# Attention and two feed-forward layers on one core: the last sixteen tiles' steps written in another order on all five engines

## The reference

```
def _layer(x, wqkv, qs, ksc, wo, lg, lb, w1, b1, w2, b2):
    h = shift_token(x)                      # half of the columns taken from the row before
    q, k, v = split(h @ wqkv)               # 256 -> 3 x 512, 8 heads of 64
    q, k = l2norm(q) * qs, l2norm(k) * ksc
    q, k = rotary_xpos(q, k)
    o = local_attention(q, k, v)            # window of 128 rows, and the window before
    x = x + o @ wo
    h = layernorm(shift_token(x)) * lg + lb
    a, g = split(h @ w1 + b1)               # 256 -> 2 x 682
    return x + (a * gelu(g)) @ w2 + b2
x = layernorm(x + attention(x)); y = x
for l in range(2): y = _layer(y, ...)
return layernorm(x + y)
```

## Time and profile before

| | us |
|---|---|
| median of 3 runs (smallest to largest) | 2690.54 (2689.98 to 2692.51) |
| the profiled execution: its time, its span | 2691.48, 2689.7 |
| TensorE busy | 2630.9 (98%) |
| VectorE busy | 2275.5 (85%) |
| ScalarE busy | 1934.2 (72%) |
| GpSimd busy | 1658.0 (62%) |
| `last_steps` on TensorE | from 2402.3 to 2684.8 |

### The profile page before, as it was taken

The page is one execution under the profiler, slowest core; times in us unless marked ns, Lnnn a source line. Parts: engine busy times, 40 slices in busy tenths (PEclk is TensorE's granted clock), DMA queues, the critical chain, the costliest instruction groups (busy, mean ns, idle before and its releaser), DMA issues. The chain is left out here.

```text
span 2689.7 us, 65519 instructions
## 1 busy us (share of the span) xinstructions
PE 2630.9 (98%) x22240; PEld 2317.6 (86%) x22240; DVE 2275.5 (85%) x6866; ACT 1934.2 (72%) x4826; POOL 1658.0 (62%) x1753
## 2 busy tenths in 40 slices
PE   8999999999999999999999999999999999999998
PEld 6677788899999899999998988989898998988887
DVE  5778888888888888888887889888989989998786
ACT  5655588777777777777776777777777777778775
POOL 6533755566566566566555676666766667766563
PEclk9999899999999999999999999999999999999999
DMA  9931200000000000000012211111110111111110
GB/s 315 341 100 54 107 21 25 28 28 25 29 25 25 28 24 29 27 27 25 28 39 90 89 36 34 33 33 37 35 32 30 37 33 37 30 36 34 30 32 23
DMA packets 144510, 140.37 MB, mean 52 GB/s; under 512 B 16024, under 2 KB 126128, under 8 KB 143408
## 3 DMA queue, kind: packets, MB, share of 16 engines
q1 hardware_dynamic: 144176, 136.18, 16.0%
HBM read 80.02 MB, written 51.92 MB: 49 GB/s over the span
## 5 line engine op out<-in xcount | busy, mean ns | idle before, releaser
L954 POOL TENSOR_TENSOR prob<-prob,rinv 128x512 f32<-128x512 f32 (+1 forms) x512 | 506.1, 1000 | 396.4 <-DVE rinv L1760 396.1
L1218 ACT ACTIVATE prob<-prob,least 128x256 f32<-128x256 f32 (+1 forms) x1024 | 495.8, 486 | 62.4 <-DVE least L1752 60.9
L932 POOL TENSOR_TENSOR inv_norm<-norm_clipped,minus_half 128x8 f32<-128x8 f32 x256 | 422.7, 1658 | 79.5 <-DVE norm_clipped L1718 72.1
L1752 DVE CUSTOM_DVE_ANT_0 prob<-p_pair,mask,inv_norm 128x256 f32<-128x256 f32 (+1 forms) x1024 | 440.2, 459 | 35.1 <-PE p_pair L176 33.2
L174 PE MATMUL p_pair<-hT_h,w_h 128*128 128x256 f32 (+1 forms) x1408 | 413.4, 294 | 8.5 <-DVE gated L1824 3.6
L176 PE MATMUL p_pair<-hT_h,w_l 128*128 128x256 f32 (+1 forms) x1408 | 394.9, 280 | 0.0
L175 PE MATMUL p_pair<-hT_l,w_h 128*128 128x256 f32 (+1 forms) x1408 | 394.5, 280 | 0.0
L1230 ACT ACTIVATE pT<-p_turn 128x512 f32<-128x512 f32 (+1 forms) x512 | 283.5, 569 | 76.6 <-PE p_turn L2529 64.1
L174 PE MATMUL p_pair<-wqkv_h,xT_h 128*128 128x512 f32 x768 | 329.6, 429 | 6.5 <-DVE rope_sin L1702 2.6
L176 PE MATMUL p_pair<-wqkv_h,xT_l 128*128 128x512 f32 x768 | 305.6, 398 | 0.0
L175 PE MATMUL p_pair<-wqkv_l,xT_h 128*128 128x512 f32 x768 | 304.6, 397 | 0.0
(11 more groups left out here) (129 smaller groups left out, 7577.4 us busy)
## 6 DMA issues: line engine op xcount, KB each, us to landing
x_tile<-x_rows SPq DMA_DIRECT2D x192, 128.0 KB, 2.1
a_wraw<-in_w_all SPq DMA_DIRECT2D x32, 264.0 KB, 5.3
w_high<-a_wraw_h SPq DMA_DIRECT2D x32, 264.0 KB, 3.9
w_low<-a_wraw_l SPq DMA_DIRECT2D x32, 264.0 KB, 4.4
a_x<-in_x SPq DMA_DIRECT2D x32, 256.0 KB, 4.2
x_rows<-a_x SPq DMA_DIRECT2D x64, 128.0 KB, 2.0
x_tile<-x_rows SPq DMA_DIRECT2D x128, 64.0 KB, 2.0
mid_rows<-x_mid SPq DMA_DIRECT2D x128, 64.0 KB, 1.7
```

What stands on the lines that cost most here:

```text
L932: pool.tensor_tensor(r[:, t.slot(2), heads], rt[:, heads], half[:, heads], ALU.pow).then_inc(pool_r[n], 1)
L954: pool.tensor_tensor(p, p, rinv[:, 2 * m:2 * m + 2].unsqueeze(2).to_broadcast([P, 2, cols.stop - cols.start]), ALU.mult).then_inc(pool_p, 1)
L1218: act.activation(prob[:, h, cols], prob[:, h, cols], ACT.Exp, bias=least[:, h:h + 1], scale=-1.0, accum_out=rsum[:, h:h + 1]).then_inc(act ...
L1752: dve.tensor_tensor_reduce(prob[:, h, cols], p_score[h % 2][:, c0 + cols.start:c0 + cols.stop], mask[:, a.slot(2), cols], r[:, a.slot(2), ...
```

## The change

The calls inside the five `last_steps` lists are written in another order. Each engine has the same calls with the same arguments as before (69 on SP, 154 on POOL, 346 on ACT, 506 on DVE, 300 on PE), and the waits (`after`) on PE move with their calls, some of them naming another step that now precedes. The beginning and the loop are untouched. The first few calls of each list are the same; the first one that differs on PE is the 43rd. The diff is some 2,300 lines long, and three pieces of it follow. On SP, the first one:

```diff
@@ -842,8 +842,8 @@
             load_x1(T(117))
             store_x(T(112))
             store_x(T(113))
+            load_x(T(120))
             store_mid(T(116))
-            load_x(T(120))
             load_shifted(T(116))
             load_x1(T(118))
             store_mid(T(117))
...
```

On DVE near the end:

```diff
             gated_low(Q(122), 5)
-            least_of(T(127), 0)
-            least_of(T(127), 1)
-            least_of(T(127), 2)
-            least_of(T(127), 3)
-            o_low(T(126))
-            x_new(T(122))
-            final_statistics(T(122))
-            least_of(T(127), 4)
-            least_of(T(127), 5)
-            inverse_sums(T(127), 0)
-            least_of(T(127), 6)
-            final(T(122))
-            least_of(T(127), 7)
-            x_new(T(123))
-            final_statistics(T(123))
-            inverse_sums(T(127), 1)
-            final(T(123))
-            middle(T(126))
-            h_affine(Q(124))
-            h_low(Q(124))
-            statistics(T(126))
-            o_low(T(127))
             normed(T(126))
             gated(Q(124), 0)
             gated(Q(124), 1)
-            middle(T(127))
+            x_new(T(122))
+            final_statistics(T(122))
+            statistics(T(127))
+            gated(Q(124), 2)
+            final(T(122))
+            x_new(T(123))
+            normed(T(127))
             gated_low(Q(124), 0)
+            final_statistics(T(123))
+            gated(Q(124), 3)
             gated_low(Q(124), 1)
-            gated(Q(124), 2)
             gated_low(Q(124), 2)
-            gated(Q(124), 3)
-            statistics(T(127))
+            h_affine(Q(126))
             gated_low(Q(124), 3)
             gated(Q(124), 4)
+            final(T(123))
             gated(Q(124), 5)
-            normed(T(127))
+            h_low(Q(126))
             gated_low(Q(124), 4)
             gated_low(Q(124), 5)
-            h_affine(Q(126))
-            h_low(Q(126))
+            gated(Q(126), 0)
             x_new(T(124))
...
```

On PE, around the place to which the output product of tile 127 has come (its own new line stands just ahead of the piece):

```diff
-            after((dve_oT, T(127), 1, 1))
-            output(T(127))
+            after((dve_gT, Q(122), HF + 1, 6))
+            narrow(T(122))
             after((dve_gt, Q(124), HF + 1, 1))
             widen(Q(124), 2)
             after((dve_gt, Q(124), HF + 1, 2))
             widen(Q(124), 3)
+            after((dve_x, T(122), 1, 1))
+            narrow(T(123))
             after((dve_gt, Q(124), HF + 1, 3))
             widen(Q(124), 4)
+            after((dve_hn, T(127), 1, 1))
+            turn_h(Q(126))
             after((dve_gt, Q(124), HF + 1, 4))
             widen(Q(124), 5)
-            after((dve_hn, T(127), 1, 1))
-            turn_h(Q(126))
-            after((dve_hv, Q(126), 1, 1))
-            narrow(T(124))
             after((dve_hT, Q(126), 1, 1))
             widen(Q(126), 0)
+            after((dve_gT, Q(124), HF + 1, 6))
+            narrow(T(124))
             after((dve_gt, Q(124), HF + 1, 6))
             widen(Q(126), 1)
+            after((dve_gt, Q(126), HF + 1, 1))
+            widen(Q(126), 2)
             after((dve_x, T(124), 1, 1))
             narrow(T(125))
-            after((dve_gt, Q(126), HF + 1, 1))
-            widen(Q(126), 2)
             after((dve_gt, Q(126), HF + 1, 2))
             widen(Q(126), 3)
             after((dve_gt, Q(126), HF + 1, 3))

...
```

More of the change, by code:

```diff
@@ L1482, in last_steps @@
             v_out(T(122))
[L1483 to L1497 removed]
+            k_high(T(122))
@@ L2107, in last_steps @@
             q_low(T(120))
             inverse_sums(T(119), 1)
-            gated(Q(116), 0)
+            rope_cos(T(121), 0)
+            norms(T(121), 0)
             x_new(T(114))
+            rope_sin(T(121), 0, 0)
+            clip(T(121), 0)
+            rope_sin(T(121), 0, 1)
             final_statistics(T(114))
+            q_sum(T(121))
+            k_low(T(120))
+            x_new(T(115))
+            final(T(114))
+            final_statistics(T(115))
+            h_affine(Q(116))
+            final(T(115))
@@ L2177, in last_steps @@
             least_of(T(121), 7)
-            gated(Q(116), 5)
-            h_affine(Q(118))
-            gated_low(Q(116), 5)
-            o_low(T(120))
-            h_low(Q(118))
+            k_low(T(122))
+            q_low(T(122))
+            x_new(T(116))
+            inverse_sums(T(121), 1)
+            final_statistics(T(116))
             rope_cos(T(123), 1)
@@ L2903, in last_steps @@
             turn_k(T(119))
+            after((act_v, T(119), 1, 1))
+            widen(Q(114), 1)
+            after((dve_mid, T(116), 1, 1))
+            turn_x(T(120))
             after((dve_gt, Q(114), HF + 1, 1))
@@ L3147, in last_steps @@
             turn_probs(T(122), 3)
+            after((act_pT, T(122), 4, 3))
+            values(T(122), 2)
+            after((dve_kr, T(124), 1, 1))
+            project_v(T(124))
             after((dve_q, T(124), 1, 1))
@@ L3263, in last_steps @@
             turn_probs(T(125), 1)
-            after((dve_mid, T(124), 1, 1))
-            turn_x(T(127))
+            after((act_pT, T(125), 4, 1))
+            after((pool_p, T(125), 4, 3))
+            turn_probs(T(125), 2)
+            after((dve_kr, T(127), 1, 1))
+            project_v(T(127))
+            after((dve_x, T(119), 1, 1))
+            turn_h(Q(122))
+            after((dve_kT, T(126), 1, 1))
+            scores(T(126), 0)
+            after((dve_q, T(127), 1, 1))
+            after((act_pT, T(125), 4, 3))
@@ L3321, in last_steps @@
             turn_probs(T(126), 0)
+            after((dve_gt, Q(120), HF + 1, 4))
+            widen(Q(120), 5)
+            after((dve_oT, T(125), 1, 1))
+            after((act_pT, T(126), 4, 1))
+            values(T(126), 0)
+            after((dve_oT, T(125), 1, 1))
+            output(T(125))
+            after((dve_kT, T(127), 1, 1))
+            scores(T(127), 0)
             after((dve_kT, T(127), 1, 1))
@@ L3376, in last_steps @@
             values(T(127), 3)
+            after((dve_gt, Q(122), HF + 1, 3))
+            widen(Q(122), 4)
+            after((dve_gt, Q(122), HF + 1, 4))
+            widen(Q(122), 5)
+            after((dve_oT, T(127), 1, 1))
+            output(T(127))
             after((dve_hT, Q(124), 1, 1))
```

1489 lines of the change are left out of this document (731 added, 758 removed).

## The result

The changed kernel takes 2696.07 us (median of 22 runs, 2689.8 to 2704.05), the kernel before 2690.43 (22 runs, 2687.49 to 2700.89). The ratio is 1.0018, with a 95% interval of 1.0011 to 1.0025: slower, by about 4.8 us, which is just under the 5.4 us that I had called the least a measurement can tell.

A forecast was written before the change was run, and what follows sets the result against it. TensorE, busy 2630.9 of 2689.7 us, bounds the kernel, so only its waits change. From the profiled 2691.48, +1.0 at the end and +0.5 in the middle give 2693.0, or 2692.0 against the median; range 2683.5 to 2699.

The forecast's parts named there:

- What bounds the kernel: Whole kernel: TensorE is busy 2630.9 of 2689.7 us, so a new order can only win back its waits.
- The end, covered turn_h, late h_low: After output(127): turn_h(126) no longer waits, widen(126,0) loses 3.35 us for h_low; 7.3 us lost against 7.1, +0.2.
- The clock at the end: After output(127): idle may halve TensorE's clock, adding 1.6 us (+1.8 in all); the middle, +1.0, was taken.
- The middle, +0.5: Tiles 112 to 127: one-hop shortfalls say +1.4 us, the saved wait for x takes 1.0 back; +0.5 likeliest.
- The wait on the transfer: turn_x(122) waits 0.86 us for x of tile 122; more TensorE work in between would save about 1.0.
- three places that I named: Middle, predicted shortfalls: probs_out(118) 1.64, project_v(122) behind gated(116,5) 1.24, project_v(125) behind v_out(124) and a squares 1.51 us.
- the count of one hop: Middle: TensorE work between dependent calls less the shortest hand-over; shortfalls sum to 4.8 us old, 6.2 new, so +1.4.
- the 13 that I had named as the sign of being wrong: TensorE idle up to output(127), before 9.2 us: above 13 (slower) or under 5 (faster) makes the prediction wrong.
- The factor of 2.5: Middle: queues adding to each other as before, 12.1 / 4.8, turn 6.2 into 15.6 us, so +3.5.
- my slow rival: ScalarE's queue at gelu(114,4) makes shortfalls compound by 2.5 or more, clock lowered at the end: 2696 to 2699; chance 0.20.
- Two loads out of the full stretch: Middle: gelu(114,4) and (114,5) share a table load; two loads leave ScalarE's crowded stretch, 2.6 us of its time.
- Theory A: From the experiments: each long wait is one call too far back in a queue; over a microsecond also lowers the clock.

The follow-up runs named there:

- e3: Kernel after with tile 119's x_low ahead of q_sum(118) and a clip on VectorE, and the end reordered on TensorE, VectorE and ScalarE; ratio 1.0011 to before.
- e7: Kernel after with GpSimd's k_sum of tile 118 cut from 128x512 to 128x64; one profile, last steps 292.0 us against 293.25 in the kernel after.
- e5: Kernel after with three exp calls moved on ScalarE (tile 120's 6 and 7, tile 123's 0), so four table loads go; ratio 1.0008 to before.
- e9: Kernel after with tile 119's x_low earlier, the end reordered, three exp calls moved, and nine more calls moved on VectorE and ScalarE; ratio 1.0008 to before.
- e1: Kernel after with one VectorE call moved: tile 119's x_low ahead of q_sum(118) and a clip; ratio 1.0020 to before.
- e2: Kernel after with narrow(123) and turn_h(126) earlier on TensorE and the calls around them on VectorE and ScalarE reordered; ratio 1.0019 to before.
- e10: Kernel before with middle(118), x_low(127) and h_affine(122) moved earlier on VectorE; ratio 0.9993 to before.
- e11: Kernel after with tile 119's x_low earlier, end reordered, three exp calls moved, and gated(116,5) and least_of(125,1) to (125,3) earlier on VectorE; ratio 0.9998 to before.

## Why the prediction was right, and which terms were off

- *What bounds the kernel.* Right: TensorE has the same work, and the change shows in its waits and, which the sum had at the end alone, in its clock.
- *The end, covered turn_h, late h_low.* The mechanism was right call by call: 0.9 us predicted before widen(124,5), 0.92 lost; 3.35 before widen(126,0), 2.88 lost; normed(127) behind x_new(123) in time. h_low started at 15.5 us after output(127) (2666.39 - 2650.89), predicted 15.85. e3 shows that VectorE's and TensorE's order there made it.
- *The clock at the end.* I took half of 1.6 us. It fell, and cost 2.75, because the slow stretch was 6 us long and not 3.3. The end came out at +2.4 instead of +1.0: a term mis-sized. The Trainium skill (TensorE: Matmul & The Clock Gate, "HAM oscillation") says that gaps of TensorE that are long enough bring it back to half the clock and are to be avoided. The trace agrees at this place: 0.51 over 6.1 us behind a wait of 2.65.
- *The middle, +0.5.* Measured +3.4, of which some 1.6 is clock. The wait on the transfer went, as said. Of the three places that I named, two came (probs_out(118): 0.54 and 0.69 idle; project_v(122) behind gated(116,5): 1.16). The third, project_v(125), has no wait of its own; TensorE had waited 1.51 us a few calls ahead of it, before turn_h(120), for the xT_l of the same tile. Not seen: the wait for xT_l of tile 119 (1.31), because I took the shortest VectorE times and two were 0.6 and 1.1 us longer beside GpSimd (e7 for the clip), and the clock there; and gated(116,4) behind a table load between single exp calls (1.39). The term that was mis-sized is the count of one hop: it summed to +1.4, and the trace gave +3.4. The idle time up to output(127), 12.4 us, is just under the 13 that I had named as the sign of being wrong.
- *The factor of 2.5* by which one-hop shortfalls grow was my slow rival: +3.5 in the middle and +1.8 at the end are 5.3 us, where the profiles show +3.4 and +2.4 and the ratio 4.8. It was nearer than the forecast, and I gave it 0.20. Its place was only partly right: gelu(114,4) costs something, but tile 119 costs more.
- *Two loads out of the full stretch* were worth nothing by themselves: the window of 2450 to 2500 has 35.92 us of ScalarE work instead of 39.71, and TensorE still loses 4.1 us in it instead of 3.3. In e5 and e9 the calls behind such a move were late for other reasons.
- *The numbers.* 4.8 us by the ratio against 1.5 forecast. The median, 2696.07, is within the range of 2683.5 to 2699, which is wide, just above the 2686 to 2696 of the forecast, and at the lower end of the slow rival; 0.18% is within 0.2% by a hair. Both terms were too small, so the number owes its place in the range to the slow rival's bound and not to the sum.

Open: why the profiled clock falls at one wait in one run and at another in the next (e1, e2 and e3 near 2566, after near 2448, before at neither). A wait of over a microsecond is not enough, as Theory A had it: in the kernel after it fell behind the waits of 1.31 and 2.65 us and not behind those of 1.38, 1.13, 1.39, 1.16, 1.51 and 2.60. No run here separates that from chance, and each profile has one draw of it, of 1.7 to 11.6 us in these kernels (an estimate: half of the time for which TensorE worked at the lower clock in the last steps). The part of one edit in a difference of 1 to 2 us is therefore read from its own waits and not from the last steps.

## What to carry to other kernels

When queues on several engines are full, a written order is worth what its single late calls are worth: read each wait on the bounding engine back to the one call that stands too far behind, and expect anything from all of the sum to nothing to stay (all 2.7 us of tile 119 in e7 up to output(127), 1.5 of 2.9 in e10, none in e11). Don't judge an order by adding "longer distances": a distance that is long on TensorE does nothing when the supplier stands behind a call that waits for something else. And price a wait with the clock that may follow it: here 2.65 us of waiting cost 2.75 more. Before a wait is said to have returned, look for it in a kernel that doesn't have the edit: the one before turn_h(120) grew by 0.8 us without any.

## What the runs showed of the hardware

- A VectorE instruction over 128x8 elements took 1.23 us beside GpSimd's tensor_tensor and 0.28 when that was cut short (e7); q_sum took 0.68 us in most cases and up to 1.24 in the kernel after, 1.50 in before. In the last steps such lengthenings (over 0.15 us above the median of the line and shape) sum to about 12.5 us in the kernel before and 15 in the kernel after.
- Which of two such rows is stretched turned on less than 0.1 us between their starts: gated_low took 1.24 us where GpSimd's k_scaled ("k_rot") had started 0.08 us ahead of it (e2), and 0.43 where it had itself started 0.01 ahead (after), with k_scaled at 1.31 instead of 1.04. That alone is 0.8 us between kernels that have the same order there.
- Runs of one and the same program differ by 7 to 14 us, and mostly go with the granted clock: of the kernel after, 2689.8 us at a mean of 0.994, 2704.05 at 0.990. By an estimate from these figures, half the clock during 5.4 us loses 2.7, which is 0.001 of the mean, so four thousandths make 10.8 us of the 14. The clock isn't all of it: other runs at 0.990 took from 2695.9 us.
